# A two-layer cross-attention kernel: row sums of the softmax taken from the second pass, and layer 0 features that arrive transposed

## The reference

```python
# layer 0, 16 heads of 32
h = concatenate([context, x], axis=1)
q, (k, v) = x @ q_w + q_b, split(h @ kv_w + kv_b)
attn = softmax(where(mask, q k^T / 32, -inf))
a = (attn v) @ out_w + out_b + x
out = gelu(rmsnorm(a) @ mlp_w1 + mlp_b1) @ mlp_w2 + mlp_b2 + x
# layer 1
a = layernorm(context)
Q, K, V = out @ Wq.T, a @ Wk.T, a @ Wv.T
out = out + tanh(gate) * (softmax(where(mask, Q K^T / sqrt(32), -inf)) V) @ Wo.T
```

## Time and profile before

| | |
|---|---|
| median of 3 runs | 2361.8 us (2361.79 to 2361.86) |
| span of the profiled execution | 2367.1 us |
| busy: PE, ACT, DVE, POOL | 99%, 63%, 49%, 13% |
| layer 0, MLP, layer 1 | about 0 to 1020, 1020 to 1760, 1760 to 2367 us |

### The profile page before, as it was taken

The page is one execution under the profiler, slowest core; times in us unless marked ns, Lnnn a source line. Parts: engine busy times, 40 slices in busy tenths (PEclk is TensorE's granted clock), DMA queues, the critical chain, the costliest instruction groups (busy, mean ns, idle before and its releaser), DMA issues.

```text
span 2367.1 us, 44011 instructions
## 1 busy us (share of the span) xinstructions
PE 2333.6 (99%) x14706; PEld 1903.5 (80%) x14706; DVE 1160.4 (49%) x2246; ACT 1480.3 (63%) x3458; POOL 299.2 (13%) x336
## 2 busy tenths in 40 slices
PE   8999999999999999999999999999999999999998
PEld 7877777777777777678888888888878888888886
DVE  7555555555666566633122122122156666666664
ACT  6777777778777777744222222222248778787876
POOL 1111110111111110410000000000131221212120
PEclk9999999999999999999999999999999999999999
DMA  7444444444444444622011011011144555545443
GB/s 211 96 112 116 116 116 107 105 106 108 107 105 107 107 115 99 173 104 76 18 53 37 16 53 40 14 53 43 46 147 128 148 134 146 137 140 146 138 127 90
DMA packets 148369, 239.11 MB, mean 101 GB/s; under 512 B 25648, under 2 KB 59856, under 8 KB 148320
## 3 DMA queue, kind: packets, MB, share of 16 engines
q1 hardware_dynamic: 146912, 238.05, 37.0%
q10 hardware_dynamic: 1408, 0.41, 0.1%
HBM read 86.28 MB, written 25.21 MB: 47 GB/s over the span
## 4 chain that ended last, share of the span: by engine, by line
PE 53%; SPq 1%; ACT 1%; DMA 1%; DVE 0%; issue 0%; DVEq 0%
PE item_ps L65 6%; PE item_ps L66 6%; PE item_ps L67 6%; PE score_ps L67 5%; PE score_ps L66 5%; PE score_ps L65 5%; PE o_ps L65 4%; PE o_ps L67 4%; PE o_ps L66 4%; PE score_ps L1475 3%; PE score_ps L1434 2%; PE o_ps L1491 2%; SPq L536 1%; PE item_ps L1324 1%; ACT score_ps L831 1%; DMA layer_result<-rows 0%
## 5 line engine op out<-in xcount | busy, mean ns | idle before, releaser
L831 ACT ACTIVATE score_ps<-score_ps,l_neg_max 128x512 f32<-128x512 f32 (+1 forms) x1024 | 568.6, 561 | 121.5 <-DVE l_neg_max L1106 119.5
L1106 DVE TENSOR_REDUCE l_neg_max<-score_ps 128x1 f32<-128x512 f32 (+1 forms) x768 | 495.9, 684 | 56.9 <-PE score_ps L1434 55.4
L1947 ACT ACTIVATE mlp_hidden<-score_ps,b_col 128x512 f32<-128x512 f32 x128 | 88.4, 691 | 503.4 <-PE score_ps L67 457.9
L1995 DVE TENSOR_TENSOR mlp_hidden_l<-mlp_hidden,mlp_hidden_h 128x512 fp32r<-128x512 f32 x128 | 92.0, 719 | 519.2 <-ACT mlp_hidden_h L1949 519.1
L65 PE MATMUL item_ps<-feats_h,weights_l 128*128 128x256 f32 (+1 forms) x1024 | 322.0, 314 | 1.7 <-PEq L1821 0.8
L852 ACT ACTIVATE l_probs<-score_ps 128x1024 f32<-128x1024 f32 x272 | 270.8, 1020 | 82.1 <-PE score_ps L1475 79.0
L66 PE MATMUL item_ps<-feats_l,weights_h 128*128 128x256 f32 (+1 forms) x1024 | 318.2, 311 | 0.0
L67 PE MATMUL item_ps<-feats_h,weights_h 128*128 128x256 f32 (+1 forms) x1024 | 317.9, 310 | 0.0
L1434 PE MATMUL score_ps<-l_stack 97*128 97x512 f32 (+1 forms) x1024 | 299.8, 360 | 13.0 <-ACT score_ps L831 7.1
L1475 PEld LDWEIGHTS score_ps<-l_stack 99*128 99x128 f32 x1536 | 214.1, 193 | 49.4 <-issue 17.2
L1475 PE MATMUL score_ps<-l_stack 99*128 99x256 f32 x1536 | 244.9, 292 | 4.0 <-ACT score_ps L831 2.4
(11 more groups left out here) (176 smaller groups left out, 4191.6 us busy)
## 6 DMA issues: line engine op xcount, KB each, us to landing
l_stack<-room SPq DMA_DIRECT2D x254, 192.0 KB, 3.2
l_stack<-l_qk SPq DMA_DIRECT2D x254, 128.0 KB
l_stack<-room SPq DMA_DIRECT2D x130, 128.0 KB, 2.9
l_stack<-l_qk SPq DMA_DIRECT2D x254, 64.0 KB
l_stack<-room SPq DMA_DIRECT2D x130, 64.0 KB, 2.9
l_tokens<-in_x SPq DMA_DIRECT2D x16, 512.0 KB, 3.4
l_tokens<-in_ctx SPq DMA_DIRECT2D x16, 512.0 KB, 4.3
l_rows<-in_x SPq DMA_DIRECT2D x16, 512.0 KB, 4.0
```

The lines of the kernel that those rows point to most:

```text
L831: m = act.activation(e, e, ACT.Exp, bias=neg_max[:, q, h:h + 1], accum_out=row_sum[:, q, h:h + 1])
L1106: dve.tensor_reduce(out, bank, AXIS_X, ALU.max, negate=True).then_inc(max_done, 1)
L1947: act.activation(hidden[:, m % HBUF, :], hidden_ps[:, m % 4, :], ACT.Gelu_apprx_tanh, bias=b1_col[:, m:m + 1])
L1995: dve.tensor_tensor(hidden_p[1][:, m % HBUF, :], hidden[:, m % HBUF, :], f32(hidden_p[0][:, m % HBUF, :]), ALU.subtract).then_inc(hidden_l ...
```

## The change

The first pass makes maxima only: `step_sum` is gone, a bank of `score_ps` is free after `step_max`, and `make_shift` has two operations instead of five. `spread_sums` and `copy_inv` are gone. The row sums now come from the exponentials of the second pass. In layer 0 GpSimd adds the first two `probs` of a group (`add_pair`, 128x1024), VectorE adds the third and the fourth (`add_rest`); in layer 1 VectorE adds the two. A matmul with a matrix of ones, in fp32 as `weigh` is, sums over the keys (`sum_probs`, four per group). ScalarE makes the reciprocal as exp(-ln(x)) (`invert`), and VectorE's `normalise` refines it in two more operations. A `probs` buffer is free only when the additions have read it.

In layer 0 the features come from the host already transposed, one block of 128 features by 512 tokens at a time (`load_block`), so the items 0 to 3 with their transposes are gone; ScalarE makes the high part from SBUF (`tokens_high`), GpSimd the low part (`split_low`), which VectorE made before. All copies of the values go to ScalarE. The second pass now holds two items instead of three and the whole of one value block (`v_ahead` with four parts instead of one); the other three are interleaved by feature block with 12 score steps. GpSimd's row scaling of layer 0 moves to the next trip, between `split_low` 1 and 2. In layer 1 `layer_norm` moves behind `o_low(3)`. The table of ScalarE functions is loaded ahead, and ln and exp are in one set.

The core of the diff:

```diff
+            def split_low(b, f):
+                pool.wait_ge(split_high_done, FB * b + f + 1)
+                pool.tensor_tensor(hT[1][:, f, :], tokens[:, f % 2, :], f32(hT[0][:, f, :]), ALU.subtract
+                                   ).then_inc(split_low_done, 1)
+
+            def add_pair(a, g):
+                pool.wait_ge(probs_ready, PSTEPS * a + KB * g + 2)
...
+                pool.tensor_tensor(total[g % 2], probs[KB * g % PROBS], probs[(KB * g + 1) % PROBS], ALU.add
+                                   ).then_inc(pair_added, 1)
...
+            def iteration(p, a, prev):
...
+                elif first and a is not None:
+                    split_low(p, 0)
+                    split_low(p, 1)
+                    if prev is not None:
+                        row_scale(prev)
+                        normalise_rows(prev)
+                    split_low(p, 2)
+                    split_low(p, 3)
...
+            def invert(a, g):
+                act.wait_ge(total_done, FB * a + g + 1)
+                at_least(act, o_norm_done, FB * a + g)
+                act.activation(log_sum, o_ps[g % 2][:, S:2 * S], ACT.Ln).then_inc(log_done, 1)
+                act.wait_ge(log_done, FB * a + g + 1)
+                act.activation(inv_sum, log_sum, ACT.Exp, scale=-1.0).then_inc(inv_made, 1)
...
+            def add_rest(a, g):
+                if first:
+                    dve.wait_ge(pair_added, FB * a + g + 1)
+                    dve.wait_ge(probs_ready, PSTEPS * a + KB * g + 3)
+                    dve.tensor_tensor(total[g % 2], total[g % 2], probs[(KB * g + 2) % PROBS], ALU.add
+                                      ).then_inc(third_added, 1)
...
             def normalise(a, g):
-                dve.wait_ge(pv_done, PSTEPS * a + KB * (g + 1))
-                dve.tensor_tensor(o_norm[:, g % 2, :], o_ps[g % 2][:, 0:S], inv_of(a)[:, g, :], ALU.mult
-                                  ).then_inc(o_norm_done, 1)
+                dve.wait_ge(inv_made, FB * a + g + 1)
+                dve.tensor_tensor(log_sum, o_ps[g % 2][:, S:2 * S], inv_sum, ALU.mult).then_inc(inv_step, 1)
+                dve.wait_ge(inv_step, 2 * (FB * a + g) + 1)
+                dve.scalar_tensor_tensor(log_sum, log_sum, 2.0, inv_sum, ALU.subtract, ALU.mult).then_inc(inv_step, 1)
+                dve.wait_ge(inv_step, 2 * (FB * a + g) + 2)
+                dve.scalar_tensor_tensor(o_norm[:, g % 2, :], o_ps[g % 2][:, 0:S], -1.0, log_sum, ALU.mult, ALU.mult
+                                         ).then_inc(o_norm_done, 1)
...
+            def sum_probs(a, g):
+                pe.wait_ge(all_added, FB * a + g + 1)
+                for j in range(HG):
+                    n = pe.matmul(o_ps[g % 2][DH * j:DH * (j + 1), S:2 * S], ones[:, :],
+                                  total[g % 2][:, S * j:S * (j + 1)], start=True, stop=True,
+                                  skip_group_check=True, tile_position=(0, DH * j))
+                n.then_inc(total_done, 1)
...
             def second_pass_of_four_keys(p, a, run, shifted, next_scores):
...
                 run(0)
                 shifted(a, 5)
                 shifted(a, 6)
-                halves = itertools.count()
-                item(p, a, MIXED + 2, lambda: between(7))
+                shifted(a, 7)
                 shifted(a, 8)
+                sum_probs(a, 0)
                 run(1)
                 shifted(a, 9)
                 shifted(a, 10)
```

More of the change, by code:

```diff
@@ L260, in attention_layer @@
     PLAIN_V = KB - 2
-    MIXED = NT + NK - 1
-    SLOT = [("share", 0)] + [("v", t) for t in range(PLAIN_V)] + [("item", k) for k in range(MIXED)]
+    MIXED = 4 if first else NT + NK - 1
+    SLOT = ([("values", f) for f in range(FB)] if first else [("share", 0)]) + [("item", k) for k in range(MIXED)]
     SLOTS = len(SLOT)
@@ L494, in v_bank @@
             return item_ps[t][:, :] if t < PLAIN_V else o_ps[t - PLAIN_V][:, :]
-        def sums_later(slot):
-            kind, n = SLOT[slot]
-            return (kind == "item" and n < NT) or (kind == "share" and not first)
         def kind_of(slot, p, a):
@@ L960, in iteration @@
                         high(p, n)
+                    if first and a is not None and 0 < slot <= FB:
+                        if slot == FB:
+                            copy_v(a, 0)
+                        if p is not None:
+                            tokens_high(p, slot - 1)
                     if a is not None and slot == VALUE_SLOT:
-                        for t in V_OF_ACT:
+                        for t in range(1 if first else 0, KB):
                             copy_v(a, t)
@@ L1215, in iteration @@
                         low(p, MIXED)
-                        low(p, MIXED + 1)
                     else:
                         ahead.first_lows(dve)
-                    normalise(a, 0)
-                    o_low(a, 0)
+                    add_rest(a, 0)
                     if p is not None:
-                        low(p, MIXED + 2)
+                        low(p, MIXED + 1)
                     else:
@@ L1225, in iteration @@
                             ahead.parts.w1_low(dve, 1, part)
-                    normalise(a, 1)
-                    o_low(a, 1)
+                    add_rest(a, 1)
+                    normalise(a, 0)
+                    o_low(a, 0)
                     if p is None:
@@ L1569, in last_batch_of_four_keys @@
                 shifted(a, 4)
-                spread_sums(a, 1)
                 shifted(a, 5)
                 run(0)
-                for s in range(6, 10):
-                    shifted(a, s)
+                shifted(a, 6)
+                shifted(a, 7)
+                shifted(a, 8)
+                sum_probs(a, 0)
                 run(1)
+                shifted(a, 9)
                 shifted(a, 10)
+                project(a, 0)
                 shifted(a, 11)
-                project(a, 0)
                 shifted(a, 12)
+                sum_probs(a, 1)
+                run(2)
                 shifted(a, 13)
-                run(2)
                 shifted(a, 14)
+                project(a, 1)
                 shifted(a, 15)
-                project(a, 1)
+                sum_probs(a, 2)
                 run(3)
                 project(a, 2)
+                sum_probs(a, 3)
                 project(a, 3)
@@ L1632, in run @@
                         weigh(a, s)
-                if last_of_first(a):
+                if first and p is None:
                     last_batch_of_four_keys(a, stack, run, my_shifted)
@@ L1648, in iteration @@
                         turn_norm(prev)
-                    if kind == "v":
-                        v_item(a, n, step)
+                    if kind == "values":
+                        values(a, n, step)
                     elif kind == "item":
                         item(p, a, n, step)
-                    if a is not None and SLOT[slot][0] == "share" and not (first and isinstance(a, int) and a == 0):
+                    if a is not None and SLOT[slot][0] == "share":
                         v_share(a, 0)
```

511 lines of the change are left out of this document (253 added, 258 removed).

## The result

The changed kernel takes 2678.7 us (median of 4 runs, 2674.2 to 2683.1) against 2361.8: 1.134 times as long (95% interval 1.132 to 1.135). The profiled execution has a span of 2679.9 us, 312.8 more than before.

A forecast was written before the change was run, and what follows sets the result against it. TensorE's own columns were taken to bound the kernel; layer 0 +145, layer 1 +129 and the clock +49 made +323 on 2367.1, 2690 us profiled, so a median of 2685 us, range 2535 to 2810.

The forecast's parts named there:

- The chain behind run 0: Layer 0, second pass: 10.4 us of serial work until project(0), against 5.5 of TensorE's own; stall 4.9 us.
- The two loops: Layer 0, from one o_high to the next, twice: 8.0 us against TensorE's 5.8; stall 2.2 us each time.
- Relief: First pass: with banks free after the maximum, waits for exponentials go; −1.0 us per layer 0 trip, −0.5 in layer 1.
- Columns: TensorE per trip: transposes and spread_sums removed, sum_probs added; net about 0 in layer 0, +1.4 us in layer 1.
- Layer 1's second pass: Layer 1: waits at the projections, run 1 and the last sum, 4.8 us per trip together.
- The layer norm: Layer 1, behind o_low(3): chain of 6.5 us against 3.0 of TensorE's work; stall 3.5 us ahead of the transposes.
- The clock: Every trip: one stretch at half TensorE clock behind stalls, 1.7 us each, 29 times, +49 us.
- A: Rival: chain of group 0 shorter than TensorE's 5.5 us, sums hidden, columns decide; about 2343 us; 8%.
- B: Rival: stalls without a slower TensorE clock; 2636 us; 20%.
- C: Rival: TensorE's clock falls again and again, three stretches per trip; 2783 us; 15%.
- E: Rival: half of the stalls, and half of the clock's 49 us, go because copies overlap more; 2522 us; 8%.
- D: Rival: GpSimd and VectorE lock each other out, additions wait in two groups per layer 0 trip; 2762 us; 5%.

The follow-up runs named there:

- the filler: Changed kernel with twelve useless matmuls of 512 columns ahead of project(0) in each layer 0 trip; ratio 1.131 to the kernel before.
- the run with all three: Changed kernel with early sums and reordered second pass in layer 0, sooner layer norm in layer 1, sooner feature requests in the head; ratio 1.085 to the kernel before.
- The attempt to win it back: Changed kernel with batch 1's first two feature blocks requested ahead of the mask and batch 0's moves; ratio 1.132 to the kernel before.

## Why the prediction was right, and where it was not

Point by point.

- **The chain behind run 0** was the main step, 10.4 us; it measured 10.2 (665.52 to 675.74). The wait of 4.9 measured 4.1 in three pieces (0.64, 0.17, 3.27), since TensorE's own work in it was 6.1 instead of 5.5. Shown by moving a link (the projection 1.6 sooner, as priced) and by shortening one (0.92 sooner).
- **The two loops**, 8.0 each, measured 9.04 and 7.95, and 7.9 and 7.9 where the filler held the clock. But the waits were 0.60 and 1.68, not 2.2 and 2.2. This term was mis-sized by 2.1 us a trip: I set the loop against TensorE's 5.8 us at full clock, and at half the clock that work takes so long (8.3 us from 675.74) that the first wait nearly goes.
- **The token copies**: 1.4 predicted, 0.40 measured (a wait for GpSimd's `split_low`).
- **Relief** of the first pass: 1.0 and 0.5 predicted, from three waits a trip. This was misread: a layer 0 trip of the kernel before holds one such wait of 0.21 us and a smaller one, 0.3 in all, and a layer 1 trip none. There was next to nothing to win.
- **Columns**: about 0 predicted in layer 0; at full clock (the shorter trips of the run with all three) TensorE's work between the waits is 62.7 us against 61.7 before. In layer 1 a cost was missing: a sum that stands alone between fp32r matmuls takes 0.57 us to the next start (2289.83 to 2290.40) and makes the `shifted` ahead of it 0.67 (2289.16 to 2289.83) instead of 0.53, while ahead of a run it takes 0.45 (668.96 to 669.41). About 0.25 for each, four times a trip, 1.0 us.
- **Layer 1's second pass**: 4.8 predicted, 1.9 measured (0.28, 0.63, 0.62 and 0.40). The chains came as priced (to `project(0)` 4.86 for 4.9, from `o_high(2)` to `project(3)` 3.48 for 3.4), but TensorE had more of its own to do meanwhile: 4.0 us instead of 3.1 ahead of `project(0)`, where the sums cost more, and six matmuls of the values ahead of `project(2)`, which I had not counted.
- **The layer norm**: 3.5 predicted, 2.88 measured. Moving it took the wait away, so its cause is shown.
- **The clock**: one stretch a trip predicted, one found. In layer 1 it costs the 1.6 us between 47.4 and 45.8 (predicted 1.7). In layer 0 the stretch is longer, 6.3 us at 0.58, but its price lay largely under the loop: a trip of the filler's run without it is only 1.1 us shorter.
- **Heads and ends**: taken as 0 with ±10, measured 34. This was a true miss. In the head (15.5) ScalarE's copies of the values stand behind feature blocks that are still on their way (the 10.91 us), and the first product waits (the 9.85 us) for weights' parts that on ScalarE stand behind the last two feature blocks of batch 0, which it got at 12.88 us. The attempt to win it back gained 2.7 us in the head and nothing that shows in the total. The 9.6 between the layers and the 8.9 at the end stay unexplained.

So the trips together were put at 323 us and measured 279, the rest of the program at 0 and measured 34: two misses of opposite sign, so that the total is nearer than its terms is in part luck. Within a trip it is the same. The stalls were put at 10.7 us in layer 0 and 8.3 in layer 1 and measured 6.8 and 4.8, and TensorE's own work (a trip less its waits, so columns and clock) was put at 1.6 and 3.1 more and measured 3.1 and 5.0 more. The path was right, the division between waiting and slower work was not. Of the rivals, A (sums hidden) failed where it said it would be decided, `o_low(0)` comes 3.27 us late. B (no slower clock) and C (three stretches) are out by the clock rows. E (half of the stalls hidden) was not far off in the waits, but wrong in the time, since the work grew. D did not decide the changed kernel: in its trips no addition was stretched (one was, in the last batch, 3.39 us at 1161.70). But it decided the run with `normalise` ahead of the additions, where one took 3.22 us beside GpSimd's in every trip. The rule of the Trainium skill behind it ("SBUF — State Buffer", Who interferes with whom) is borne out. In the changed kernel, too, a subtraction of 128x16 on VectorE takes 1.22 us beside GpSimd and 0.17 without it:

```profile
655.81 1.22 DVE L1124 TENSOR_TENSOR l_shift<-l_neg_max,l_shift 128x16 fp32r<-128x16 f32 x1
...
654.45 2.55 POOL L768 TENSOR_TENSOR l_rows<-l_rows,l_bo 128x512 f32<-128x512 f32 x2 [12.37 <-DMA l_rows<-in_x]
...
717.98 0.17 DVE L1124 TENSOR_TENSOR l_shift<-l_neg_max,l_shift 128x16 fp32r<-128x16 f32 x1
```

In the run with the sooner layer norm such a lock (1.27 instead of 0.42) stood on the chain and cost 0.85 us of the wait at the last projection.

## What to carry to other kernels

When a value that was made early is to be made late, write down the serial chain behind it on all engines, in the order of their queues, and set it against the work that the bounding engine still has; shares of busy time can't tell. A link that gets shorter pays only if nothing behind it takes the gain back, be it an operation that now runs beside another engine's (3.22 us instead of 1.23) or a slower clock that falls where nothing hides it (1.4 us): follow the gain to the end of the trip before it is counted. And try the halves of a change apart: here the one that removed columns was worth 0.7% once its low parts went to an idle engine, while the whole cost 13%. The late sums alone on the kernel before were not run, so that they cost the difference is argued, from the runs that moved their chain.

## What the runs showed of the hardware beyond what I expected

Behind the long waits (3.27 us in layer 0, 2.88 in layer 1) TensorE went from 2.4 to 1.2 GHz (granted clock 0.50) for some 3.4 to 6.7 us; useless matmuls in the wait of layer 0 kept it at 2.4 GHz there, and it fell later in the trip instead, without a gain that shows in the total, because the chain set the pace. A short fp32 sum between fp32r matmuls cost about 0.25 us beside its columns. And a VectorE operation with two inputs in SBUF took as long as the GpSimd operation beside it let it: 1.22 us instead of 0.17 for 16 columns, 3.22 instead of 1.23 for an addition of 1024.
